# One opening block for an eight-layer kernel: x in quarters, weight loads, clearing, the first layer norm and the combined weights

## What is computed

```python
x = L0_attn_x                                  # (1, 2048, 128)
x = x + _L0_attn_ref(_layernorm(x), L0_attn_W_disp, L0_attn_W_val, L0_attn_rel_pos_emb, ...)
x = x + _L0_ffn_ref(_layernorm(x), ...)
...                                            # six more of the same form, up to _L3_ffn_ref
return x
```

## Time and profile before

| | |
|---|---|
| median of 3 runs | 2984.93 us |
| the three runs | 2976.29, 2984.93, 2985.98 us |
| the profiled execution | 2982.17 us, of which the span of instructions is 2980.4 us |
| TensorE busy | 2389.2 us (80%) |
| ScalarE busy | 2010.5 us (67%) |
| VectorE busy | 1860.6 us (62%) |
| GpSimd busy | 1070.7 us (36%) |
| mean granted TensorE clock | 0.907 of full speed |

### The profile page before, as it was taken

The page is one execution under the profiler, slowest core; times in us unless marked ns, Lnnn a source line. Parts: engine busy times, 40 slices in busy tenths (PEclk is TensorE's granted clock), DMA queues, the critical chain, the costliest instruction groups (busy, mean ns, idle before and its releaser), DMA issues. The chain is left out here.

```text
span 2980.4 us, 33149 instructions
## 1 busy us (share of the span) xinstructions
PE 2389.2 (80%) x12605; PEld 833.9 (28%) x12605; DVE 1860.6 (62%) x2713; ACT 2010.5 (67%) x2036; POOL 1070.7 (36%) x408
## 2 busy tenths in 40 slices
PE   3677777757666666766999889998769789999995
PEld 1122222334222222333222241222434422222223
DVE  5788898857999999864888528896350401112114
ACT  4999999813633333234899758997431379999991
POOL 5999999711099999531001300013000000000000
PEclk8899999978888888787999998999889889999997
DMA  2012111110144444102202100101010120210001
GB/s 75 1 43 62 67 43 43 43 53 8 28 176 168 163 162 152 68 4 78 41 12 37 35 7 1 18 6 45 8 40 0 35 65 18 41 27 18 15 6 28
DMA packets 64985, 144.64 MB, mean 49 GB/s; under 512 B 13091, under 2 KB 27791, under 8 KB 64112
## 3 DMA queue, kind: packets, MB, share of 16 engines
q1 hardware_dynamic: 64816, 142.40, 16.5%
HBM read 117.92 MB, written 24.25 MB: 48 GB/s over the span
## 5 line engine op out<-in xcount | busy, mean ns | idle before, releaser
L674 POOL TENSOR_TENSOR l0a_diff_pool<-l0a_A,l0a_a_of_t 128x2048 f32<-128x2048 f32 x128 | 531.7, 4191 | 34.3 <-ACT l0a_a_of_t L689 33.0
L1933 ACT ACTIVATE l2x_pT<-ps 128x1024 f32<-128x1024 f32 x512 | 495.7, 1021 | 14.5 <-PE ps L1892 12.6
L1933 ACT ACTIVATE l3he_pT<-ps 128x1024 f32<-128x1024 f32 x512 | 496.0, 1021 | 6.5 <-PE ps L1892 4.6
L1262 PE MATMUL ps<-l1s_hc,all_ident 128*128 128x512 f32 x512 | 288.7, 718 | 153.2 <-POOL l1s_hc L1233 97.6
L657 DVE SCALAR_TENSOR_TENSOR l0a_diff_dve<-l0a_A,l0a_pos,ps 128x512 f32<-128x512 f32 x512 | 344.8, 741 | 29.7 <-PE ps L532 29.7
L1224 POOL TENSOR_TENSOR l1s_dBx<-l1a_dtx,l1a_Bs 128x1024 f32<-128x1024 f32 x128 | 297.7, 2357 | 111.9 <-POOLq L958 111.9
L1248 ACT ACTIVATE ps<-l1a_dt,l1a_A 128x1024 f32<-128x1024 f32 x128 | 143.0, 1118 | 268.0 <-DVE l1s_hc L1307 215.7
L1892 PE MATMUL ps<-l2m_Qs,l2m_Ks 75*128 75x512 bf16 x1024 | 273.9, 392 | 9.8 <-PEq L2215 9.8
L1892 PE MATMUL ps<-l3h_Qs,l3h_Ks 75*128 75x512 bf16 x1024 | 269.3, 386 | 12.8 <-DVE ps L1981 12.8
L1906 PE MATMUL ps<-l2x_pT,l2m_Va 128*9 128x512 f32 x2048 | 272.5, 605 | 1.2 <-ACT l2x_pT L1933 1.2
L1906 PE MATMUL ps<-l3he_pT,l3h_Va 128*9 128x512 f32 x2048 | 269.2, 598 | 0.6 <-ACT l3he_pT L1933 0.6
(11 more groups left out here) (462 smaller groups left out, 3347.8 us busy)
## 6 DMA issues: line engine op xcount, KB each, us to landing
l1a_Bs<-l1a_bc SPq DMA_DIRECT2D x64, 512.0 KB, 3.6
l1s_Cs<-l1a_bc SPq DMA_DIRECT2D x64, 512.0 KB, 4.8
l0a_band_rows<-l0a_band SPq DMA_DIRECT2D x32, 512.0 KB, 5.2
l0a_band<-l0a_exps SPq DMA_DIRECT2D x16, 512.0 KB, 5.1
l2m_Ks<-l2m_parts SPq DMA_DIRECT2D x36, 128.0 KB
l2m_Qs<-l2m_parts SPq DMA_DIRECT2D x72, 64.0 KB
l3h_Qs<-l3h_parts SPq DMA_DIRECT2D x72, 64.0 KB
l0a_band<-l0a_zero SPq DMA_DIRECT2D x8, 512.0 KB, 4.8
```

What stands on the lines that cost most here:

```text
L674: pool.tensor_tensor(out, window(s), atb[:, p % 2, :].unsqueeze(1).broadcast_to([P, 4, CH]), ALU.subtract).then_inc(diff_pool, 1)
L1262: mm = pe.matmul(g.ps[:, (4 + 2 * h + q) * CH:(5 + 2 * h + q) * CH], g.ident[:, :], hc[:, m % NHC, q * CH:(q + 1) * CH], start=(n == 0), s ...
L1933: act.activation(pT[:, turn % NPT, :], g.ps[:, slot * QC:(slot + 1) * QC], ACT.Exp).then_inc(expd, 1)
```

## The change

x is loaded by four DMAs, one for each four blocks, each with a semaphore of its own, and block 1 no longer waits for them; VectorE waits for a quarter ahead of its statistics. Blocks 2, 3 and 4 become one. In it SyncE first issues the eleven weight loads and then, after `zero` is cleared, the eight writes of zeros. The layer norm is the class `LayerNorm`, in PSUM banks 4 to 7. TensorE waits for all weight loads, transposes W_disp, transposes the normalised x, and then does the products. VectorE clears the tiles, does the layer norm, and does the building and the W_disp copy (`combine`) between its normalised blocks and its copies of quarters 1 and 3; the reducers and the last copies follow. GpSimd's mask `bm` has a semaphore `head_mask`, for which `combine` waits.

```diff
--- before.py
+++ after.py
@@ -66,13 +66,15 @@
     g.ones = r.sb("ones", [P, P])
     g.eps = r.sb("eps", [P, 1])
     g.ps = ctx.enter_context(nc.psum_tensor("ps", [P, 8 * CH], F32))
-    x_loaded, zeroed, ready = r.sem("x_loaded"), r.sem("ident_zeroed"), r.sem("consts_ready")
+    g.x_loaded = [r.sem("x_loaded%d" % q) for q in range(NCH)]
+    zeroed, ready = r.sem("ident_zeroed"), r.sem("consts_ready")
     with nc.Block() as block:
 
         @block.sync
         def _(sp):
-            sp.dma_start(g.X[:, :, :], x_dram.rearrange("a (b p) c -> p (a b) c", p=P)).then_inc(x_loaded, 16)
-            sp.wait_ge(x_loaded, 16)
+            rows = x_dram.rearrange("a (b p) c -> p (a b) c", p=P)
+            for q in range(NCH):
+                sp.dma_start(g.X[:, 4 * q:4 * q + 4, :], rows[:, 4 * q:4 * q + 4, :]).then_inc(g.x_loaded[q], 16)
 
         @block.gpsimd
         def _(pool):
@@ -214,10 +216,12 @@
                 self.copy(act, act.copy, 0)
         self.copy(act, act.copy, 2)
 
-    def vector(self, dve, meanwhile=None):
+    def vector(self, dve, meanwhile=None, x_loaded=None, between=None):
         step = Steps(dve, self.steps)
         ve, sd, rs, tmp = self.ve, self.sd, self.rs, self.tmp
         for b in range(TB):
+            if x_loaded is not None and b % 4 == 0:
+                dve.wait_ge(x_loaded[b // 4], 16)
             last = dve.bn_stats(self.st[:, b, :], self.g.X[:, b, :])
         step(last)
         for b in range(TB):
@@ -235,6 +239,8 @@
         dve.scalar_tensor_tensor(self.nm[:, :], self.mv[:, :, 0], -1.0, rs[:, :], ALU.mult, ALU.mult).then_inc(self.scale_ready, 1)
         for b in range(0, TB, 2):
             dve.tensor_scalar(self.xn[:, b, :], self.g.X[:, b, :], self.mv[:, b, 0:1], rs[:, b:b + 1], ALU.subtract, ALU.mult).then_inc(self.norm[0], 1)
+        if between is not None:
+            between()
         for q in range(1, NCH, 2):
             self.copy(dve, dve.tensor_copy, q)
 
@@ -309,17 +315,19 @@
                 ld(bdo[:, :], I["L0_attn_b_dmg_out"].rearrange("(a b) -> a b", b=1).broadcast_to([P, 1]))
                 return n
 
-            sel, zr = r2.sem("mask_steps"), r2.sem("zeroed")
+            sel, zr, head_mask = r2.sem("mask_steps"), r2.sem("zeroed"), r2.sem("head_mask_ready")
+            built, tr_ps, tr_sb = r2.sem("blocks_built"), r2.sem("wd_transposed"), r2.sem("wdT_copied")
+            comb, pos_ps = r2.sem("weights_combined"), r2.sem("pos_in_psum")
+            ln = LayerNorm(nc, g, ctx2, "ln0", load, 4)
             with nc.Block() as block:
 
-                @block.vector
-                def _(dve):
-                    dve.memset(zero[:, :], 0.0).then_inc(zr, 1)
-                    dve.memset(wbs[:, :, :, :], 0.0)
-                    dve.memset(A[:, :, :, 0:PAD], 0.0)
-                    dve.memset(V[:, :, :, HS:HS + 1], 1.0)
-                    dve.memset(VS[:, :, :, HS:HS + 1], 1.0)
-                    dve.memset(VS[0:W, 0, :, 0:HS], 0.0)
+                @block.sync
+                def _(sp):
+                    ln.sync(sp)
+                    sp.wait_ge(zr, 1)
+                    for par in range(2):
+                        for b in range(4):
+                            sp.dma_start(band[par, b], zero[:, :]).then_inc(band_zeroed, 16)
 
                 @block.gpsimd
                 def _(pool):
@@ -329,30 +337,23 @@
                                        pattern=[[-BD, HH]], channel_multiplier=1).then_inc(sel, 1)
                     pool.wait_ge(sel, 2)
                     pool.affine_select(out=bm[:, :], in_=bm[:, :], compare_op=ALU.is_ge, fill=0.0, base=BD - 1,
-                                       pattern=[[BD, HH]], channel_multiplier=-1)
+                                       pattern=[[BD, HH]], channel_multiplier=-1).then_inc(head_mask, 1)
                     pool.memset(early[:, :], 0.0).then_inc(sel, 1)
                     pool.wait_ge(sel, 3)
                     pool.affine_select(out=early[:, :], in_=early[:, :], compare_op=ALU.is_ge, fill=NEG, base=1 - W,
                                        pattern=[[1, W]], channel_multiplier=1)
 
-                @block.sync
-                def _(sp):
-                    sp.wait_ge(zr, 1)
-                    for par in range(2):
-                        for b in range(4):
-                            sp.dma_start(band[par, b], zero[:, :]).then_inc(band_zeroed, 16)
-
-            layernorm_transpose(nc, g, "ln0", load)
-
-            built, tr_ps, tr_sb = r2.sem("blocks_built"), r2.sem("wd_transposed"), r2.sem("wdT_copied")
-            comb, comb_sb, pos_ps = r2.sem("weights_combined"), r2.sem("weights_copied"), r2.sem("pos_in_psum")
-            with nc.Block() as block:
+                @block.scalar
+                def _(act):
+                    ln.scalar(act)
 
                 @block.tensor
                 def _(pe):
+                    ln.loaded(pe)
                     for hf in range(2):
                         mm = pe.transpose(g.ps[:, hf * P:(hf + 1) * P], wd[:, hf * P:(hf + 1) * P], g.ident[:, :])
                     mm.then_inc(tr_ps, 1)
+                    ln.tensor(pe)
                     pe.wait_ge(built, 1)
                     pe.matmul(g.ps[:, 2 * CH:2 * CH + W], wposr[:, :, :].rearrange("k h c -> k (h c)"), relT[:, :],
                               start=True, stop=True).then_inc(pos_ps, 1)
@@ -365,13 +366,25 @@
 
                 @block.vector
                 def _(dve):
-                    for k in range(2):
-                        dve.tensor_tensor(wblk[:, k, :].rearrange("p (h c) -> p h c", c=BD),
-                                          wrep[:, k, :].unsqueeze(1).broadcast_to([P, HH, BD]),
-                                          bm[:, :].unsqueeze(2).broadcast_to([P, HH, BD]), ALU.mult)
-                    dve.tensor_copy(wposr[:, :, :], wpos[:, :].unsqueeze(1).broadcast_to([BD, HH, BD])).then_inc(built, 1)
-                    dve.wait_ge(tr_ps, 1)
-                    dve.tensor_copy(wdT[:, :, :].rearrange("p h c -> p (h c)"), g.ps[:, 0:2 * P]).then_inc(tr_sb, 1)
+                    dve.memset(zero[:, :], 0.0).then_inc(zr, 1)
+                    dve.memset(wbs[:, :, :, :], 0.0).then_inc(zr, 1)
+                    dve.memset(A[:, :, :, 0:PAD], 0.0)
+                    dve.memset(V[:, :, :, HS:HS + 1], 1.0)
+                    dve.memset(VS[:, :, :, HS:HS + 1], 1.0)
+                    dve.memset(VS[0:W, 0, :, 0:HS], 0.0)
+
+                    def combine():
+                        ln.loaded(dve)
+                        dve.wait_ge(head_mask, 1)
+                        for k in range(2):
+                            dve.tensor_tensor(wblk[:, k, :].rearrange("p (h c) -> p h c", c=BD),
+                                              wrep[:, k, :].unsqueeze(1).broadcast_to([P, HH, BD]),
+                                              bm[:, :].unsqueeze(2).broadcast_to([P, HH, BD]), ALU.mult)
+                        dve.tensor_copy(wposr[:, :, :], wpos[:, :].unsqueeze(1).broadcast_to([BD, HH, BD])).then_inc(built, 1)
+                        dve.wait_ge(tr_ps, 1)
+                        dve.tensor_copy(wdT[:, :, :].rearrange("p h c -> p (h c)"), g.ps[:, 0:2 * P]).then_inc(tr_sb, 1)
+                    ln.vector(dve, None, g.x_loaded, combine)
+                    dve.wait_ge(zr, 2)
                     for k in range(2):
                         for n in range(4):
                             dve.tensor_scalar(wbs[:, k, n, 8 * n:8 * n + 8], bm[:, :], wo[:, k:k + 1], None, ALU.mult)
```

## The result

The changed kernel takes 2971.45 us in the median (17 runs, 2964.41 to 2983.95), the kernel before 2986.47 on the same chips (17 runs, 2976.29 to 3002.49). The ratio is 0.9952, 95% interval 0.9939 to 0.9965: 14.3 us less, 10.5 to 18.2. The forecast was 2972.0, and faster by more than 0.3% at a chance of 0.64. The ratio is the time of a kernel divided by that of the kernel before.

A forecast was written before the change was run, and what follows sets the result against it. GpSimd paces the first layer, so only the 31.77 us opening can shrink: 4.1 from not waiting for x plus 6.2 from the merged block gives 10.3, and 2982.3 - 10.3 = 2972.0 us; range 2964.1 to 2980.

The forecast's parts named there:

- The bound: First layer runs at GpSimd's pace once its main block starts at 31.77 us; moving that start moves everything after.
- One sign of being wrong: Distance from the main block's first matmul to the end of the span; anything but 2948.6 us would be wrong.
- Step 1: Block 1: x in four issues, no wait; the merged block starts at 3.6 us instead of 7.75, gaining 4.1.
- Step 2: VectorE's layer norm: statistics from 6.4 us, first normalised block at 12.35, all eight of VectorE's at 14.5.
- Step 3: Weight loads in the merged block: last lands at 14.65, 11.03 after first issue, allowing 1 less to 1.5 more.
- Step 4: Weights' landing to end of merged block: TensorE's transposes, then copies; main block starts at 21.45, TensorE's combining hidden.
- The sum: Main block's first matmul moves from 31.77 to 21.45 us, a gain of 10.3.
- B: Rival, clogged DMA queue: x's quarters issue at 0.96 each, first loads stand behind; gain 8 to 9, chance 0.20.
- C: Rival, x's quarters land one after another with their own latency, last at 13.3; gain 7.8, chance 0.04.
- D: Rival, weight loads land 3 us early, SyncE's issues set the floor at 19.5; gain 12.2, chance 0.10.
- A: The main forecast for the opening: gain 10.3 us, bounds 9 to 11.5, chance 0.58.
- E: Rival, TensorE's clock takes the gain back: 22 groups at the lower level cost 19 us, 9 slower; chance 0.08.

The follow-up runs named there:

- block1_waits: Changed kernel with block 1 waiting for all four quarters of x; ratio 0.9972 against the kernel before.
- zeros_first: Changed kernel with the eight writes of zeros issued ahead of the eleven weight loads; ratio 1.0001 against the kernel before.
- clearing_on_gpsimd: Changed kernel with b_dmg_out loaded early, reducers made early, a semaphore for W_disp, and the clearings of A, V and VS on GpSimd; ratio 0.9929.
- whole_x: Changed kernel with x in one DMA again, still no wait in block 1; ratio 0.9952 against the kernel before.
- bdo_first: Changed kernel with the load of b_dmg_out issued first of the eleven; ratio 0.9955 against the kernel before.
- the last three versions: Changed kernel with b_dmg_out and reducers early, adding in turn a W_disp semaphore, clearings on GpSimd, zero writes in the main block; ratios 0.9941, 0.9929, 0.9928.
- after: First profiled execution of the changed kernel, no further edit; 2976.24 us profiled, median 2971.45 us over 17 runs.
- after_again: The changed kernel run a second time with no edit; ratio 0.9960 against the kernel before.

## Why the prediction was right

**The bound.** What the opening gives up moves the first layer as a whole: block1_waits passed 3.8 us on unchanged, zeros_first gave 11 us back and the ratio went to 1.0001, and the first layer took 587.6 to 589.7 us in twelve of thirteen profiled executions, wherever it began. The three variants whose main block starts more than 3 us later than the changed kernel's (24.6, 27.7, 31.9) have the higher ratios in the same order (0.9972, 0.9993, 1.0001), though neighbouring intervals overlap. One sign of being wrong that the prediction named did come: from the main block's first matmul to the end there are 2954.7 and 2955.5 us in the changed kernel's two executions, not 2948.6. It doesn't decide anything, since this distance has 2950.0 in the second execution of the kernel before and lies anywhere from 2944.1 (block1_waits) to 2958.2 (clearing_on_gpsimd).

**Step 1** had the block start at 3.6; it was 3.30, since the first issue took no longer than the rest (2.09 for four). The claim that the quarters themselves give little held (whole_x, 0.9952).

**Step 2** had the statistics from 6.4 and normalised x at 12.35; they came at 6.00 and 11.89, the 0.3 of step 1 and 0.1 to 0.2 more.

**Step 3**, the wait for the loads, was right in mechanism and place and 1.26 us too long: 13.07 - 3.30 = 9.77 from first issue to TensorE, not 11.03. The eleven issues take 6.12 (3.30 to 9.42) instead of 7.73, the difference lying mostly in the first two of them, which had stood behind the zeros (0.86 and 1.19 then, 0.34 and 0.42 now). The lower allowance of 1 us less was too narrow.

**Step 4** had 6.8 us from landing to the main block; 13.07 to 19.73 is 6.66. The sixteen transposes took 3.23, 0.2 each, as taken from L354's row. In the second execution this step took 7.76 (13.04 to 20.80): the combining matmuls ended at 19.76 and VectorE's last copy waited 0.61 for them, the case that the prediction named and left unpriced.

**The sum**: 21.45 was forecast, 19.73 measured; of the 1.7 us, 1.26 are step 3, 0.3 step 1, 0.14 step 4. The rest of the larger gain, 1.4 us in the profiled execution, is L457 at the upper clock (3.67, not 5.08), which the sum had at nothing and which was absent in the second execution (5.67). The second execution's main block, at 20.80, is 0.65 us from the forecast; there step 4 took 0.96 longer than forecast, out of the 1.6 that steps 1 to 3 had won. As a time the forecast is 0.55 us off the median, closer than its reasoning deserves: a gain too small by 2 to 4 us and a kernel before taken 4 us too fast cancel.

**The rivals.** B and C fell with the timeline (the first five loads issue in 0.34 to 0.43 right behind x; statistics without a gap; the quarters' latencies overlap, for on GpSimd's clearing the statistics run from 4.69 without a gap too). The Trainium skill, page "DMA: Bandwidth & Descriptors", section "Anatomy of one DMA", counts some 2.0 us of fixed cost for one DMA, under a heading that speaks of DMAs issued by GpSimd, while these are issued by SyncE. No run here shows such a cost added up over four DMAs in flight, and its row here is the missing gap in the statistics. D, early loads, was half true: the last load landed 1.26 us sooner, not 3. The 12.04 us by which the main block came earlier in the first execution (31.77 to 19.73) lie outside A's 9 to 11.5 and beside D's 12.2, but D's floor, SyncE's issues, is not what was reached: they were over at 15.20, since the zeros issued in 5.73 and not in 7.66, and the block went on to 19.4 with VectorE's copies. The second execution, 10.97, lies within A. E, the clock, moves the opening by 3 us between two executions of one program and the first layer by 6 in one of thirteen, but no shift of 19 us was seen, and the medians don't show it taking the gain.

## What to carry to other kernels

Blocks put together run in parallel only as far as the queue allows: in the merged block the SyncE order decides, and what the first waiting engine needs has to be issued first (11 us hung on two lines here). A semaphore of its own for the operand that heads a queue, instead of a wait for all loads, takes the loads off that queue; it pays only when nothing behind it sets the same pace (here ScalarE's blocks did, and by itself it gave nothing). Judge a change of 0.5% at the place it touches and by the median of many runs; the ends of two single profiles can differ by as much as the change.

## What the hardware showed unexpectedly

A load of one float to 128 partitions (`b_dmg_out`) lands 3.3 to 3.65 us after its issue is over (3.3 in the earlier trace rows; 20.58 to 24.13 in zeros_first; 9.42 to 13.07 in the changed kernel); the one of `b_dmg`, 16 floats repeated eight times, 2.9. It isn't the only late one, as bdo_first's expectation had it: W_disp, 128 KB issued first behind x, lands 3.4 to 3.8 us after its issue is over (3.64 to 7.40, 7.31 and 7.00 in the last three versions). While the small loads were the last outstanding in the kernel before, the DMA share was 0.05, about one of sixteen engines at work:

```profile
25.00:26.00 1.00, 1.00 (x7) 0.99 (x6) 0.68 (x3) 1.00 (x4) 0.00 (x0) 1.00 0.05 0
```

The same eight zero writes were issued in 5.73, 5.08, 5.05 and 5.05 us in after, after_again, whole_x and block1_waits, and in 7.59 to 7.89 in the nine other profiled executions. In those four, and only there, the load of `b_dmg_out` is issued directly ahead of them. The faster issue moved no bytes sooner: in the changed kernel the DMA share is 0.05 to 0.07 from 10 to 12 us, though the writes are in issue since 9.47, and a write lands 7.4 us after its issue in the median; in bdo_first the share is 0.54 from 11.0 to 11.5, and a write lands after 6.0. So the small load ahead seems to hold the writes back; by what means is open.

TensorE's rate in the opening changes between executions of one program, and the granted clock in the windows doesn't always say so. In the second execution of the changed kernel:

```profile
17.68 2.08 PE L364 MATMUL ps<-l0w_wblk,l0w_wdT 128*128 128x128 f32 x8
...
20.80 5.67 PE L457 MATMUL ps<-all_hT,l0a_wcomb 128*128 128x512 f32 x8 [1.04 <-PEq L322]
```

and in the windows:

```profile
20.00:22.00 2.00, 1.21 (x2) 0.72 (x3) 0.49 (x1) 0.00 (x0) 0.00 (x0) 1.00 1.03 422
```

Eight combining matmuls took 2.08 there and 1.16 in the first execution, L457's first ones twice as long, while the granted clock stands at 1.00 from 20 to 22 us. Of the ten profiled executions with a merged block seven show 2.08 and three 1.16 to 1.20. Which of the two comes when stayed open; it costs 3 us in the opening (the first L687 at 24.97 and 28.04), more than any of the last three versions wins.
